# Attention and mixture of experts in one kernel: the two heads of a pair in the two halves of TensorE's rows, maxima taken over two banks at once, value products every step

## The reference, cut to what matters

```python
# x: 1 x 2048 x 256; 16 heads of 16 numbers; float32
q = heads(x @ Wq);  c_kv = x @ Wkv_down                 # latent of 64
k = heads(c_kv @ Wk_up);  v = heads(c_kv @ Wv_up)
q[..., 4:], k[..., 4:] = rope(q[..., 4:]), rope(k[..., 4:])
scores = where(causal, -inf, q @ k.T / 4)               # 16 x 2048 x 2048
x = layernorm(x + softmax(scores) @ v)
# then: gate over 16 experts, the best two of them a token (swiglu, 256 -> 176 -> 256),
# two shared experts, layernorm(x + both)
```

## Time and profile before

| | |
|---|---|
| time, median of 3 runs | 789.13 us (788.01 to 790.67) |
| the profiled execution, its own time | 787.88 us |
| its span | 786.1 us |
| PE busy | 699.7 us, 4086 instructions |
| DVE busy | 567.3 us |
| ACT busy | 397.4 us |
| first score (unit 0) | 51.91 us |
| unit 13 to unit 14, from one copy of value sums (L870) to the next | 437.27 to 484.05 us |

### The profile page before, as it was taken

One profiled execution on the slowest core, in us unless ns is written; L12 is line 12 of the kernel. 1 busy time (PEld: TensorE's weight loads), 2 busy tenths in 40 slices (PEclk: granted clock), 3 DMA queues, 4 the chain that ended last, 5 costly groups with the idle time before them and its releaser, 6 DMA issues.

```text
span 786.1 us, 13117 instructions
## 1 busy us (share of the span) xinstructions
PE 699.7 (89%) x4086; PEld 444.5 (57%) x4087; DVE 567.3 (72%) x1297; ACT 397.4 (51%) x848; POOL 240.3 (31%) x297
## 2 busy tenths in 40 slices
PE   3579899899999999999999999999979999999910
PEld 3456575565665556556654555554467777777710
DVE  6666679778879977787698888863687755555545
ACT  2225365455656666667666776766823232222204
POOL 6526173440072207010611000010147413333332
PEclk9759899899999999999999999999999999999965
DMA  4864315035015101500341265332332223333254
GB/s 138 204 172 109 83 43 148 24 103 119 1 42 148 56 1 41 121 2 1 93 89 65 65 215 189 126 97 57 87 98 102 90 83 95 108 108 108 87 187 160
DMA packets 45096, 75.94 MB, mean 97 GB/s; under 512 B 5695, under 2 KB 23359, under 8 KB 44863
## 3 DMA queue, kind: packets, MB, share of 16 engines
q1 hardware_dynamic: 37423, 57.55, 27.2%
q0 software_dynamic: 4896, 13.67, 5.0%
q10 hardware_dynamic: 2720, 4.00, 1.4%
HBM read 41.91 MB, written 32.93 MB: 95 GB/s over the span
## 4 chain that ended last, share of the span: by engine, by line
PE 70%; DVE 16%; DMA 4%; issue 4%; ACT 3%; ACTq 1%; POOL 0%; SPq 0%; POOLq 0%; DVEq 0%
PE banks_ps L1144 15%; PE banks_ps L1124 14%; PE banks_ps L1085 14%; PE banks_ps L1181 7%; DVE mx L1342 6%; PE banks_ps L1215 5%; PE banks_ps L1001 3%; PE banks_ps L1092 2%; PE banks_ps L1194 2%; DMA q_stack<-m_rows 2%; PE banks_ps L1228 1%; ACT probs L888 1%; PE banks_ps L1277 1%; PE banks_ps L1203 1%; DVE base L1809 1%
## 5 line engine op out<-in xcount | busy, mean ns | idle before, releaser
L1342 DVE TENSOR_REDUCE mx<-banks_ps 128x1 f32<-128x512 f32 (+3 forms) x640 | 346.6, 602 | 93.1 <-PE banks_ps L1085 50.1
L888 ACT ACTIVATE probs<-banks_ps 128x512 f32<-128x512 f32 (+3 forms) x640 | 304.1, 546 | 180.9 <-PE banks_ps L1124 166.6
L1124 PE MATMUL banks_ps<-q_stack,k_stack 98*128 98x512 f32 (+3 forms) x640 | 244.9, 399 | 15.5 <-ACT probs L888 7.2
L1085 PE MATMUL banks_ps<-k_stack,q_stack 96*128 96x512 f32 (+3 forms) x640 | 237.0, 400 | 7.3 <-DMA q_stack<-kq_split 3.4
L1085 PEld LDWEIGHTS banks_ps<-k_stack,q_stack 96*128 96x128 f32 x640 | 124.8, 198 | 82.0 <-DVE mx L1342 37.1
L1124 PEld LDWEIGHTS banks_ps<-q_stack,k_stack 98*128 98x128 f32 x640 | 122.4, 195 | 51.4 <-ACT probs L888 29.1
L741 POOL TENSOR_SCALAR_AFFINE_SELECT probs<-probs 128x512 f32<-128x512 f32 x64 | 41.0, 640 | 331.0 <-ACT probs L888 331.0
L1144 PE MATMUL banks_ps<-probs,v_ones 128*17 128x512 f32 (+3 forms) x1280 | 134.1, 536 | 1.0 <-POOL probs L741 1.0
L798 POOL DMA_INDIRECT token_y<-ys,dest x47 | 45.4, 966 | 79.2 <-DVE ys L1785 76.3
L1144 PEld LDWEIGHTS banks_ps<-probs,v_ones 128*17 128x17 f32 x1280 | 29.5, 97 | 64.9 <-issue 41.1
L1181 PE MATMUL banks_ps<-w_up_sb,xg_t 128*128 x188 | 63.8, 462 | 0.3 <-ACT xg_t L941 0.3
(11 more groups left out here) (186 smaller groups left out, 685.0 us busy)
## 6 DMA issues: line engine op xcount, KB each, us to landing
kq_split<-kq_stage SPq DMA_DIRECT2D x32, 256.0 KB, 3.4
k_stack<-kq_split SPq DMA_DIRECT2D x8, 768.0 KB, 6.6
q_stack<-kq_split SPq DMA_DIRECT2D x32, 192.0 KB, 6.1
xg<-slot_x SPq DMA_DIRECT2D x47, 130.0 KB, 2.1
slot_x<-blank SPq DMA_DIRECT2D x11, 520.0 KB, 6.9
w_up_sb<-w_up SPq DMA_DIRECT2D x16, 352.0 KB
kq_split<-kq_stage SPq DMA_DIRECT2D x32, 128.0 KB, 3.2
x_raw<-xT SPq DMA_DIRECT2D x4, 512.0 KB, 5.7
```

Source lines behind the costliest of these rows:

```text
L888: nc.scalar.activation(probs[:, s % PROB_BUFS, h, off:CH], score_bank(n)[:, off:CH], ACT.Exp)\
L1085: ins = nc.tensor.matmul(dst[:, at:at + keys], q_stack[0:STACK, u % 4, h, tile * P:(tile + 1) * P], k_stack[0:STACK, pair, kb * CH + k0:kb ...
L1124: nc.tensor.matmul(score_bank(n)[:, off:CH], k_stack[:, 2 * g + h // 2, b * P:(b + 1) * P], q_stack[:, u % 4, h, off:CH], start=True, stop ...
L1342: last = nc.vector.tensor_reduce(mx[:, u % 2, h * TPC + tile, kb:kb + 1], bank_of(bank)[:, at:at + keys], AX.X, ALU.max)
```

## The change

- The two heads of a pair stand in the two halves of the array's rows: rows 0 to 49 and rows 64 to 113 (48 rows of products, two of maxima and ones). `q_stack` shrinks to two slots of 512 a unit; the zeros go away. A max bank or a score block of a head takes 48 or 50 rows in its half in place of 96 or 98. Loads of `k_stack`, and of the rows of ones, become two transfers for one.
- Banks of maxima become pairs of banks, one a head of the pair, in two neighbouring turns. The matmuls of the two heads alternate; then both masks. VectorE takes both banks in one instruction where they are neighbours in PSUM, and in two where the pair falls on the fourth and the first bank. One pair now is a turn of two banks, and waits for the last readers of both.
- TensorE's order in a step: half of the pairs, heads 0 and 1, jobs, half of the pairs, heads 2 and 3, jobs, and then the value products of the step before, in every step.

```diff
-ROWS = STACK + 2
+ROWS = SPLIT + 2
+HALF_ROWS = P // 2
...
-        filled.append(filled[-1] + BANKS_A_STEP[u // UNITS_PER_CHUNK])
+        filled.append(filled[-1] + BANKS_A_STEP[u // UNITS_PER_CHUNK] / 2)
...
+        wide = 2 if turn in max_no else 1
+        turn_banks[turn] = [(at + k) % TURN_BANKS if n < first_alone else LAST_MAX_BANKS + at % 2 for k in range(wide)]
+        turn_before[turn] = [user.get(bank) for bank in turn_banks[turn]]
...
-                if u == 0:
-                    sp.wait_ge(zeros_low, 1)
-                if u == 2:
-                    sp.wait_ge(zeros_high, 1)
...
-                    sp.dma_start(k_stack[0:STACK, 4 * m:4 * m + 4, c * CH:(c + 1) * CH].bitcast(F32),
-                                 kq_dram[c, n - 1].rearrange("two copy (d j) n -> (two copy d) j n", j=GH)).then_inc(k_stacked, 16)
+                    for par in range(2):
+                        sp.dma_start(k_stack[half_rows(par, SPLIT), 4 * m:4 * m + 4, c * CH:(c + 1) * CH].bitcast(F32),
+                                     kq_dram[c, n - 1, par].rearrange("copy (d j) n -> (copy d) j n", j=GH)).then_inc(k_stacked, 16)
...
                 for tile, k0, keys, at in parts:
-                    ins = nc.tensor.matmul(dst[:, at:at + keys], q_stack[0:STACK, u % 4, h, tile * P:(tile + 1) * P],
-                                           k_stack[0:STACK, pair, kb * CH + k0:kb * CH + k0 + keys],
...
+                    for par in range(2):
+                        ins = nc.tensor.matmul(bank_of(of, par)[:, at:at + keys],
+                                               q_stack[half_rows(par, SPLIT), u % 4, pair, tile * P:(tile + 1) * P],
+                                               k_stack[half_rows(par, SPLIT), stacked, kb * CH + k0:kb * CH + k0 + keys],
...
-                nc.tensor.matmul(score_bank(n)[:, off:CH], k_stack[:, 2 * g + h // 2, b * P:(b + 1) * P],
-                                 q_stack[:, u % 4, h, off:CH], start=True, stop=True).then_inc(pe_scores, 1)
+                nc.tensor.matmul(score_bank(n)[:, off:CH], k_stack[half_rows(h % 2), 2 * g + h // 2, b * P:(b + 1) * P],
+                                 q_stack[half_rows(h % 2), u % 4, h // 2, off:CH], start=True, stop=True).then_inc(pe_scores, 1)
...
-                banks, jobs = quarters(max_at[s]), quarters(aux_at[s], 2)
+                banks, jobs = quarters(max_at[s], 2), quarters(aux_at[s], 2)
                 for half in range(2):
-                    for h in (2 * half, 2 * half + 1):
-                        run_banks(banks[h])
-                        if s < NS:
-                            score_head(s, h)
+                    run_banks(banks[half])
+                    if s < NS:
+                        score_head(s, 2 * half)
+                        score_head(s, 2 * half + 1)
                     for job in jobs[half]:
                         run_aux(job)
-                    if half and s % 2 == 0 and 2 <= s <= NS:
-                        values(s - 2)
+                    if half and 1 <= s <= NS:
                         values(s - 1)
...
+                for tile, _, keys, at in bank_parts(of):
+                    n, other = mx_row_of(pair, 0, tile), mx_row_of(pair, 1, tile)
+                    b0, b1 = turn_banks[of]
+                    if b1 == b0 + 1:
+                        last = nc.vector.tensor_reduce(mx[:, u % 2, n:other + 1:other - n, kb:kb + 1],
+                                                       turn_ps[:, b0:b1 + 1, at:at + keys], AX.X, ALU.max)
+                    else:
+                        for k, to in enumerate((n, other)):
+                            last = nc.vector.tensor_reduce(mx[:, u % 2, to, kb:kb + 1], bank_of(of, k)[:, at:at + keys], AX.X, ALU.max)
```

132 lines of the change are left out of this document (67 added, 65 removed).

## The result

The changed kernel takes **830.16 us** (median of four runs, 823.45 to 833.26) against 789.62 us for the kernel before on the same chip (788.01 to 790.67): a ratio of 1.0504, with a 95% interval of 1.0432 to 1.0575. It is 5% slower; 773 was forecast, and the range ended at 808. The profiled execution took 832.15 us. Mean granted clock of TensorE over its span: 0.869, against 0.951 in the kernel before.

The account below looks back on a forecast made before the run. The prediction took TensorE to bound the full step, at 2.895 us. Its terms, -5 - 1.5 - 4 + 3 - 5 - 2.4 - 1, summed to -16 us: 772 from the profiled 787.9, 773 as median, range 757 to 808.

Parts of the forecast that it names:

- The wait before head 3: In each full step TensorE stands some 0.5 us before head 3's score, until head 0's exponential frees a score bank.
- the full step: Attention step with maxima, 95 in all: from 2.895 to 2.84 us each, -5 us together.
- The last unit: Attention's last unit, without maxima: steps of 2.02 us with ScalarE running through, 12 x -0.2 = -2.4 us.
- the last of the rivals: Waits of 0.5 us in each step drop TensorE to 1.2 GHz, doubling its streams: over 850 us; chance 0.03.
- Edge of a unit: Last three steps of a unit and the next one's first: 9.95 us for 10.4, -5 us over 11 edges.
- Maxima over two banks: One VectorE instruction for two banks saves some 0.07 us per instruction less; -1 to -2 us, in the early stretch.
- Value products each step: Starting and switching come in every step, not every second: 1.39 us for 1.13, 0.26 more a step on TensorE.
- Masks: Own-key banks: two switches and two masks, 0.35 us a pair; -0.13 in three steps of 11 units, -4 us.
- The start: Maxima of unit 0 need 8 VectorE instructions less on the chain: -1 us.
- Steps with three pairs: Every fourth step of chunk 1 has a third pair awaiting the first one's banks, taking 3.6 us: +3 us.
- the halves don't stream together: Rival: a pair's matmuls run in turn, a full step takes 3.08 us, the kernel 812 us; chance 0.13.
- switches cost more: Rival: switches of tiling cost 0.1 to 0.2 us more a step, full step 2.94 to 3.04, kernel 786 to 802; chance 0.24.

Follow-up runs that it names:

- filler: Changed kernel with the matmuls of the pairs before heads 2 and 3 done three times, except a chunk's own keys: 814.29 us, ratio 1.0126 to the kernel before.
- before_ring_two: Kernel before with its ring of three score banks held as if it had two, adding waits for exponentials: 829.78 us, ratio 1.0334.
- wide_only: Kernel before with maxima in pairs of banks, heads two and two, and the wide VectorE instruction, in the 96-row layout: 842.25 us, ratio 1.0518.
- wide_narrow: wide_only with a separate VectorE instruction for each bank of a pair: 841.76 us, ratio 1.0495 to the kernel before.
- before_values_each: Kernel before with value products after every step instead of every second one: 803.91 us, ratio 1.0030.
- one_half: Changed kernel with both heads of a pair read from the first half of the rows, so they cannot stream together: 1054.1 us, ratio 1.3000 to the kernel before.
- before_short: Kernel before with odd heads' maximum and score matmuls in banks of earlier keys cut from 512 to 128 columns from unit 4 on: 804.88 us, ratio 1.0034.
- after_again: Changed kernel, unaltered, run again on the experiments' chip: 842.71 us, ratio 1.0516 to the kernel before.

## Why the prediction was wrong

**Right, with their sizes.** The price of a pair (0.234 forecast, 0.23 to 0.24 measured); the efficiency of the Trainium skill that I weighed against it (TensorE: Matmul & The Clock Gate, "Measured speedup vs the span model"), by which a pair would cost some 0.30 as an estimate, is not borne out for two halves. The wait before head 3 (0.5 forecast; the load is idle 0.66, and still 0.19 in `filler`, where the wait is filled) and with it the full step (2.84, 2.83) and the wait of ScalarE (0.7, 0.77). VectorE's 15 us. The last unit (-2.4; 35.82 against 38.14 is -2.3). The stretch of unit 13 near 45 us holds once the clock does, in `filler` (45.6). The value products start 0.43 after the last score, where I had said that more than 0.4 would speak against me: the switch costs 0.1 more than the 0.32 of before, and in the full step the other terms make up for it. That the step came out at 2.83 for 2.84 is in this part luck.

**The step that failed** is the last of the rivals: "it held full clock through the waits of the last unit", a chance of 0.03 for the falling clock. I took waits of the kernel before as the test and looked at their length only. In the last unit of before, TensorE streams scores of 98 rows between waits; in the kernel after a matmul has 48 or 50 rows, and two of them take the time of one. And I looked for the fall in full steps, where the clock in fact holds; it falls mostly near the edges between units, where the earlier trace rows had shown a fall of the kernel before. There TensorE waits for VectorE to free banks, and the next 3 to 24 us are at 1.2 GHz: 147 us of attention after, 14 before, by the estimate above 49 us, where my sum had nothing for it. The rival's "over 850" was too high for the same reason, as its mechanism was every step and not eleven stretches. The Trainium skill has this pattern (TensorE: Matmul & The Clock Gate, "A second HAM failure mode: psum-queue depth-cycling"): frequent small stands between groups of matmuls make the clock go back and forth. The traces agree for the kernel after; `before_ring_two`, with such stands and the clock at 0.938, shows that they are not enough by themselves.

**Terms that were mis-sized.** *Edge of a unit*, -5: I summed matmuls and latencies and left out that a pair claims two of four banks. `wide_only` prices that at 5% in the old form. In the new one it doesn't reach the full steps, but it stands at the edges (0.79 and 0.72 us for VectorE), and it is the likely reason why the three units 8, 10 and 11, at full clock (0.99 in the last), take 110.7 us together, against 110.9 before, where my terms gave some 4 less. *Maxima over two banks*, -1.5: too small to be told by `wide_only` against `wide_narrow`, which show no gain. *Value products each step*, +0.26 a step: 0.17 in `before_values_each`, and no measurable change of its time. *Masks*, 0.35 a pair: 0.42, as the mask starts 0.44 after its pair (512.02, 512.46) and the score 0.21 later; a step with two masked pairs takes 3.25 us against 2.83 (value products at 511.04 and 514.29), 0.42 more, where before paid 0.48: 33 steps make -2, not -4. *The start*, -1: the first score stands at 52.4 us for 51.91, so +0.5. *Steps with three pairs*, +3, no run measured by themselves. With the edge and the maxima at nothing the sum is -5 - 2 + 3 - 2.3 + 0.5 = -6 (an estimate), near the 5 us that the estimate from the clock leaves: little of the 16, even at full clock.

**The rivals.** That the halves don't stream together is refuted. That switches cost more holds in small: 0.43 for 0.32 before value products and 0.42 for 0.35 a masked pair, both inside the step of 2.83 and the 3.25 above, and neither is what made the kernel slower. That the wait before head 3 is absent is refuted. The falling clock happened, in another place and of another size.

**What stays open.** How idle time and rows combine, and why the edge at 427 us of the kernel after is followed by a fall and the edge at 266, with TensorE as little busy, is not. No run had pairs in two halves and no stand at all; `one_half` and `before_short` each change more than one thing. That the pairing of banks starts the falls at the edges of the kernel after is read from its trace; a version of it with more shared banks was not tried.

## What to carry to other kernels

Work saved on TensorE is worth what the next wait leaves of it, and can be worth less than nothing: where the time saved becomes a stand, the clock may fall and stay low for several steps (3 to 24 us here). So read the granted clock of before and after by stage, look at what stands before each fall and not at the average step, and when such a change disappoints, put matmuls back into the wait and see whether the kernel gets faster. Halving the time of a piece while doubling its claim on a ring (two of four banks) is a change to the ring too, and has to be priced there.

## What the runs showed of the hardware

- 100 us in which TensorE was shown busy without a break, with scores and maxima in one half of the rows, ran at 1.2 GHz (`one_half`), which I had not expected of an engine busy 50.00 of 50 us.
- TensorE was busy 1.73 of 3 us at full clock in the kernel before, and no fall followed.
- Adding 408 matmuls made a kernel 3.7% faster (`filler` against `after_again`).
- Alternating a 48-row matmul with 98- and 128-row ones costs 0.2 us at each change (0.43 for 0.234), while two 48-row matmuls in different halves start together.
- TensorE can wait 0.40 to 0.68 us for an exponential before three of the eight scores of two steps and keep 2.4 GHz (`before_ring_two`, 0.938 over the whole kernel, 0.943 without).
